# Which engine issues the context and V transfers beside the mixing stages: SyncE or ScalarE

## What is computed

```
x = L0(x, ctx)          # RWKV: mixing of neighbouring rows, recurrence over 112 steps, channel mix
x = L1(x, ctx, ctx)     # two cross-attentions of 16 heads x 128, then an MLP
x = L2(ctx, x, mask)    # attention of x over the context and itself, then an MLP
x = L3(x, ctx)          # attention of one head over the context

# of L0
x5  = xn[:, :, None] + sx[:, :, None] * (maa_stack + tanh(...) @ maa_w2)   # five mixes
r, k, v, g = x5[3] @ Wr.T, x5[0] @ Wk.T, x5[2] @ Wv.T, silu(x5[4] @ Wg.T)
s   = a + w * s ;  out = r . (u * a + s)                                   # a = k_t v_t
x   = x + (groupnorm(out) * g) @ Wo.T
kk  = square(relu(xk @ ffn_Wk.T)); x = x + sigmoid(xr @ ffn_Wr.T) * (kk @ ffn_Wv.T)

# of the first cross-attention of L1
vh  = (ctx @ wv1 + bv1).reshape(b, t, 16, 128)      # needs nothing of L0
```

## Time and profile before

| | |
|---|---|
| median of 3 runs | 3551.27 us |
| lowest, highest | 3536.88, 3551.39 us |
| the profiled execution: its time | 3549.67 us |
| its span | 3548.3 us |
| mean granted TensorE clock | 0.948 |
| busy: PE, DVE, ACT, POOL | 3189.4, 1486.5, 1238.4, 1109.2 us |
| chunk loads, V stores | 128 pairs, 96 |

### The profile page before, as it was taken

How to read it: one execution, slowest core, us unless ns; L and a number is a source line. 1 busy time by engine, 2 the same in 40 slices (tenths; PEclk the granted TensorE clock), 3 DMA queues, 4 the chain that set the end, 5 groups by cost and what they waited for, 6 DMA issues and landing times.

```text
span 3548.3 us, 43193 instructions
## 1 busy us (share of the span) xinstructions
PE 3189.4 (90%) x15928; PEld 2639.5 (74%) x15928; DVE 1486.5 (42%) x3184; ACT 1238.4 (35%) x2797; POOL 1109.2 (31%) x986
## 2 busy tenths in 40 slices
PE   5688978878699999999999999999899998988988
PEld 2454555556698989898989888888688777767876
DVE  4588349721333333343333333334211665662133
ACT  3222323232333333453222232223333555553322
POOL 5545335432322222332121121222342222234410
PEclk7799989989899999999999999999899999988999
DMA  6575357534333433342221121221111110101122
GB/s 226 173 217 160 118 164 223 160 110 135 117 130 122 139 128 117 129 141 73 81 86 65 65 94 65 83 80 49 36 60 58 37 37 23 39 15 54 57 82 91
DMA packets 142062, 358.25 MB, mean 101 GB/s; under 512 B 13008, under 2 KB 82128, under 8 KB 133024
## 3 DMA queue, kind: packets, MB, share of 16 engines
q1 hardware_dynamic: 141376, 354.81, 30.2%
q10 hardware_dynamic: 480, 0.69, 0.1%
HBM read 314.81 MB, written 40.63 MB: 100 GB/s over the span
## 4 chain that ended last, share of the span: by engine, by line
PE 66%; DVE 9%; ACT 7%; POOL 6%; DMA 6%; issue 4%; SPq 1%; POOLq 0%; ACTq 0%; DVEq 0%
PE bank L176 19%; PE bank L178 18%; PE bank L177 18%; PE bank L1728 5%; POOL W_lo L216 3%; DMA W_lo<-ctx_split 2%; PE bank L1713 1%; DMA W_raw<-in_weights 1%; ACT W_hi L207 1%; PE bank L620 1%; ACT prob L2408 1%; DVE prob_T_lo L256 1%; DVE max L1921 1%; ACT prob L1810 1%; DVE K_lo L258 1%
## 5 line engine op out<-in xcount | busy, mean ns | idle before, releaser
L2002 POOL TENSOR_SCALAR prob<-prob,inverse 112x376 f32<-112x376 f32 x256 | 143.5, 579 | 1124.6 <-DVE inverse L1927 1124.6
L216 POOL TENSOR_TENSOR W_lo<-W_raw,W_hi 128x1024 fp32r<-128x1024 f32 x138 | 331.1, 2421 | 192.6 <-ACT W_hi L207 190.3
L176 PE MATMUL bank<-ctx_hi,W_hi 128*128 128x376 f32 x1024 | 356.7, 348 | 26.0 <-DVE K_lo L258 20.2
L176 PE MATMUL bank<-W_hi 128*128 128x512 f32 (+2 forms) x608 | 282.8, 465 | 88.2 <-DMA W_lo<-ctx_split 49.8
L258 DVE SCALAR_TENSOR_TENSOR K_lo<-bank,vectors,K_hi 128x375 fp32r<-128x375 f32 (+1 forms) x288 | 173.8, 607 | 438.7 <-ACT K_hi L249 438.4
L177 PE MATMUL bank<-ctx_lo,W_hi 128*128 128x376 f32 x1024 | 346.0, 338 | 0.0
L178 PE MATMUL bank<-ctx_hi,W_lo 128*128 128x376 f32 x1024 | 345.4, 337 | 0.0
L176 PE MATMUL bank<-act_hi,W_hi 128*128 128x448 f32 x800 | 312.9, 391 | 29.0 <-POOLq L333 10.9
L177 PE MATMUL bank<-act_lo,W_hi 128*128 128x448 f32 x800 | 300.1, 375 | 0.0
L178 PE MATMUL bank<-act_hi,W_lo 128*128 128x448 f32 x800 | 299.8, 375 | 0.0
L249 ACT ACTIVATE K_hi<-bank,vectors 128x375 fp32r<-128x375 f32 (+1 forms) x288 | 163.4, 576 | 287.9 <-PE bank L178 287.8
(11 more groups left out here) (252 smaller groups left out, 6999.6 us busy)
## 6 DMA issues: line engine op xcount, KB each, us to landing
W_raw<-in_weights SPq DMA_DIRECT2D x69, 1024.0 KB, 5.0
ctx_hi<-ctx_split SPq DMA_DIRECT2D x64, 752.0 KB, 5.6
ctx_lo<-ctx_split SPq DMA_DIRECT2D x64, 752.0 KB, 7.1
v_spread<-v_rows SPq DMA_DIRECT2D x128, 224.0 KB
W_hi<-ctx_split SPq DMA_DIRECT2D x128, 188.0 KB, 3.3
W_lo<-ctx_split SPq DMA_DIRECT2D x128, 188.0 KB, 4.6
values<-value_rows SPq DMA_DIRECT2D x64, 256.0 KB
V<-values SPq DMA_DIRECT2D x32, 512.0 KB, 4.1
```

The source lines that it names most:

```text
L176: nc.tensor.matmul(dst, left[0], right[0], start=first, stop=False)
L216: pool.tensor_tensor(k.Wl[:, slot, cs, :], k.Wraw[:, cs, :], k.Wh[:, slot, cs, :].bitcast(F32), ALU.subtract).then_inc(*k.w_low.now((n, i)))
L2002: pool.tensor_scalar(k.Pm[:, h, :], k.Pm[:, h, :], k.rsum[:, h:h + 1], 1.0, ALU.mult, ALU.mult).then_inc(*k.prob_done.now((n, h)))
```

## The change

All chunk loads after those of the first context, and all stores of the V thirds, are issued by ScalarE. `act_fill` first loads the chunks that TensorE read at the point before, then stores the thirds that ScalarE copied out at the point before, then copies out as before. `act_values_end` stores as well. SyncE keeps the first context's chunks (`sp_first_chunks`), the weights, the spreads and the rest; its weight loads keep their places in the recurrences, and follow each other without fills between them in the mixing stage and in the channel mix. Nothing else moves: what is waited for, the lag of one point, the buffers and the transfers' shapes are the same.

```diff
 def act_fill(k, point):
     act = k.nc.scalar
+    for n in range(made_until(point, 2), made_until(point, 1)):
+        f, q = divmod(n, NQ)
+        j, c = QUANTA[q]
+        if j == 2 and f + 1 < len(FILLS):
+            act_chunk(k, f + 1, c)
+    for n in range(tiles_of(made_until(point, 3)), tiles_of(made_until(point, 2))):
+        act_value_store(k, n)
     for n in range(tiles_of(made_until(point, 2)), tiles_of(made_until(point, 1))):
         act_value_out(k, n)
...
 def act_values_end(k):
+    for n in range(tiles_of(made_until(POINTS[-1], 2)), tiles_of(made_until(POINTS[-1], 1))):
+        act_value_store(k, n)
     for n in range(tiles_of(made_until(POINTS[-1], 1)), len(TILES)):
         act_value_out(k, n)
+        act_value_store(k, n)
-def sp_fill(k, point):
...
-def sp_chunk(k, f, c):
-    sp, b = k.nc.sync, f % B
-    if f:
-        sp.wait_ge(*(k.chunk_read[f - 1, c] if c < C - 1 else k.banks.filled(("vf", f - 1, 2))))
+def act_chunk(k, f, c):
+    act, b = k.nc.scalar, f % B
+    act.wait_ge(*(k.chunk_read[f - 1, c] if c < C - 1 else k.banks.filled(("vf", f - 1, 2))))
     ch, cl = context_chunk(k, c)
-    sp.dma_start(ch.bitcast(F32), k.cx_dram[b, 0, :, c]).then_inc(k.chunk_loaded[c], 16)
-    sp.dma_start(cl.bitcast(F32), k.cx_dram[b, 1, :, c]).then_inc(k.chunk_loaded[c], 16)
+    act.dma_start(ch.bitcast(F32), k.cx_dram[b, 0, :, c]).then_inc(k.chunk_loaded[c], 16)
+    act.dma_start(cl.bitcast(F32), k.cx_dram[b, 1, :, c]).then_inc(k.chunk_loaded[c], 16)
-def sp_value_store(k, n):
+def act_value_store(k, n):
...
-    sp.wait_ge(*k.banks.drained(("vf", f, j)))
-    sp.dma_start(k.v1_dram[g, b, k0:k0 + kn], k.Vst[0:kn, n % 2, :]).then_inc(k.value_kept[n % 2], 16)
+    act.wait_ge(*k.banks.drained(("vf", f, j)))
+    act.dma_start(k.v1_dram[g, b, k0:k0 + kn], k.Vst[0:kn, n % 2, :]).then_inc(k.value_kept[n % 2], 16)
...
+def sp_first_chunks(k):
+    sp = k.nc.sync
+    for c in range(C):
+        ch, cl = context_chunk(k, c)
+        sp.dma_start(ch.bitcast(F32), k.cx_dram[0, 0, :, c]).then_inc(k.chunk_loaded[c], 16)
+        sp.dma_start(cl.bitcast(F32), k.cx_dram[0, 1, :, c]).then_inc(k.chunk_loaded[c], 16)
... in sp_rwkv:
             sp_load_weight(k, w["r"])
-            for s in range(14):
-                sp_fill(k, ("pre", 1, s))
-                if s == 5:
-                    sp_load_weight(k, w["v"])
-                if s == 10:
-                    sp_load_weight(k, w["g"])
-            sp_load_weight(k, w["o"])
+            for name in "vgo":
+                sp_load_weight(k, w[name])
...
-            sp_fill(k, ("rec", half, n))
... in sp_ffn:
-    for s in range(24):
-        sp_fill(k, ("ffn", s))
-        if s == 2:
-            sp_load_weight(k, W_FFN["fv"])
-        if s == 16:
-            sp_load_weight(k, W_X[0]["q"])
-    sp_values_end(k)
-    for w in "ko":
+    sp_load_weight(k, W_FFN["fv"])
+    for w in "qko":
         sp_load_weight(k, W_X[0][w])
```

More of the change, by code:

```diff
@@ L451, in act_values_end @@
 def act_values_end(k):
+    for n in range(tiles_of(made_until(POINTS[-1], 2)), tiles_of(made_until(POINTS[-1], 1))):
+        act_value_store(k, n)
     for n in range(tiles_of(made_until(POINTS[-1], 1)), len(TILES)):
         act_value_out(k, n)
-def sp_fill(k, point):
[L457 to L463, removed]
-def sp_chunk(k, f, c):
-    sp, b = k.nc.sync, f % B
-    if f:
-        sp.wait_ge(*(k.chunk_read[f - 1, c] if c < C - 1 else k.banks.filled(("vf", f - 1, 2))))
+        act_value_store(k, n)
+def act_chunk(k, f, c):
+    act, b = k.nc.scalar, f % B
+    act.wait_ge(*(k.chunk_read[f - 1, c] if c < C - 1 else k.banks.filled(("vf", f - 1, 2))))
     ch, cl = context_chunk(k, c)
-    sp.dma_start(ch.bitcast(F32), k.cx_dram[b, 0, :, c]).then_inc(k.chunk_loaded[c], 16)
-    sp.dma_start(cl.bitcast(F32), k.cx_dram[b, 1, :, c]).then_inc(k.chunk_loaded[c], 16)
-def sp_value_store(k, n):
-    sp, (f, j) = k.nc.sync, TILES[n]
+    act.dma_start(ch.bitcast(F32), k.cx_dram[b, 0, :, c]).then_inc(k.chunk_loaded[c], 16)
+    act.dma_start(cl.bitcast(F32), k.cx_dram[b, 1, :, c]).then_inc(k.chunk_loaded[c], 16)
+def act_value_store(k, n):
+    act, (f, j) = k.nc.scalar, TILES[n]
     (g, b), k0, kn = FILLS[f], KTILES[j][0], kept_rows(j)
-    sp.wait_ge(*k.banks.drained(("vf", f, j)))
-    sp.dma_start(k.v1_dram[g, b, k0:k0 + kn], k.Vst[0:kn, n % 2, :]).then_inc(k.value_kept[n % 2], 16)
-def sp_values_end(k):
-    for n in range(tiles_of(made_until(POINTS[-1], 2)), len(TILES)):
-        sp_value_store(k, n)
+    act.wait_ge(*k.banks.drained(("vf", f, j)))
[6 more added lines that the diff above has]
+        sp.dma_start(cl.bitcast(F32), k.cx_dram[0, 1, :, c]).then_inc(k.chunk_loaded[c], 16)
 def sp_learned(k):
@@ L1284, in sp_rwkv @@
                 sp.wait_ge(k.cx_stored[s], 32 * B)
-            for c in range(C):
-                sp_chunk(k, 0, c)
+            sp_first_chunks(k)
         pending = {}
@@ L1301, in sp_rwkv @@
                 sp_load_weight(k, pending[n])
-        if half:
-            sp_fill(k, ("post", 1))
 def plan_ffn(k):
```

## The result

| | before | after |
|---|---|---|
| median, lowest, highest of 4 runs, us | 3550.42 (3536.88, 3551.39) | 3603.31 (3600.66, 3606.64) |
| ratio, 95% interval | | 1.016 (1.014 to 1.018) |
| span and mean clock of the profiled execution | 3548.3 us, 0.948 | 3605.3 us, 0.940 |

The change makes the kernel 53 us slower. The prediction had said 26 us: the direction was right, the size was under half. The time is still inside the range on record. Two of the eleven executions of weights_later_again took 5985 and 7471 us and are left out of its ratio, not of its median.

A forecast was written before the change was run, and what follows sets the result against it. TensorE was taken to bound the mixing stages, with TensorE and VectorE close in the recurrences. Terms 21 + 11 + 6 - 10 - 10 - 4 + 12 = +26 us on the median 3551.3 gave 3577 us, range 3545 to 3615.

The forecast's parts named there:

- The rival that a DMA issue passes a waiting copy: ScalarE's loads go out while the copy ahead still waits, so all lateness is gone: about 3535 us; chance 0.05.
- the lateness: ScalarE's loads leave late behind waiting work: +21 us in the mixing stage, +11 us in the channel mix.
- the chunk behind the weight: Mixing stage: a chunk behind a 1 MB weight kept TensorE 4.52 us; in another queue it gains 4 us.
- the sign on record: Mixing stage: TensorE waits 25 us or more for chunks, in waits of 3 to 4 us, if the forecast is right.
- the step on TensorE's clock: Eight new stalls over 3 us each cost up to 3 us of low clock; half of 0 to 24 taken, +12 us.
- The even rival: Clock does not fall and mixing places overlap (15 instead of 21): +8 us, 3559 us; chance 0.24.
- the held loads: Recurrences: loads that SyncE issued late, at 491 and 515 us, go out earlier from ScalarE: -10 us.
- the queues: Recurrences: chunks in another queue need not stand behind spreads and weights: -10 us.
- The queue rival: A queue of its own saves chunks 1.5 to 2 us each: -24 us, 3527 us; chance 0.09.
- + 6: Recurrences: loads behind a gate or norm evacuation are 1 to 2 us late, four or five times: +6 us.
- issues and stores: 124 load pairs (93 us) and 96 stores (41 us) move into ScalarE's idle time and cost nothing themselves.
- the slowest rival: ScalarE's waits delay initial states, gates and V copies; 0.4 us per step, 128 steps: +51, 3628 us; chance 0.08.

The follow-up runs named there:

- weights_later_again: Kernel before with SyncE's g, fv and q weight loads asked for later, run again with more rounds: 3540.04 us, ratio 0.9981.
- loads_ahead_both: Changed kernel with ScalarE's loads and stores put ahead of the waiting copies in mixing stage and channel mix: 3557.50 us, 1.0032 of the kernel before.
- rec_only: Kernel before with the loads and stores of the two recurrences alone issued by ScalarE: 3549.18 us, ratio 1.0018.
- weights_later: Kernel before with SyncE's g, fv and q weight loads asked for at later points: 3537.99 us, ratio 0.9983.
- no_loads: Kernel before without chunk loads after the first context, whose chunks make the V of the seven others: 3507.69 us, ratio 0.9900.

## Why the prediction was right and where it failed

**Right: the place.** The prediction rested on ScalarE's order, in which each load stands behind a copy that waits for VectorE. The timeline shows it to 0.01 us, and loads_ahead_both, which moves the loads ahead of the copies in both stages, gives back four fifths of the loss. The rival that a DMA issue passes a waiting copy is refuted by the same rows. The Trainium skill (Advanced Engine Details and Errata, Sequencer Loop) lets an instruction of the engine wait in a queue while control instructions run; in this trace a DMA issue behind a waiting ScalarE copy did not run ahead of it, at 387.21, 397.70 and 408.00.

**Right: the lateness.** Forecast were 21 us for the mixing stage, less 4 for the chunk behind the weight: 17. TensorE's idle time rose by 15.9. Forecast for the channel mix were 11; it rose by 13.8. The sizes of single waits were off: eight waits in the mixing stage, as forecast, but one of 5.93 us and seven of 1.3 to 2.8, 21.2 us in all, where the sign on record was 25 us or more in waits of 3 to 4. The 9.40 us on a V copy became an 11.60 us wait for the chunk that now leaves behind eight copies, at 822.17. (The 3.9 us that the prediction had there are 3.8 by its own numbers.)

**Failed: the step on TensorE's clock, +12 us.** The mechanism was there and it was mis-sized: it is 25.1 us in the mixing stage and 8.2 in the channel mix, 33 in all. I had taken a price of up to 3 us from a single stall of 4.52 us with full work behind it, gave it only to stalls over 3 us, eight of them although its own average for the mixing stage was 2.7, and took half. The price held on the average: 25.1 us over the eight chunk waits of the mixing stage are 3.1 each. The half and the condition did not, since seven of the eight are under 3 us. Six of them come in pairs 7 to 8 us apart (392.84 and 400.59, 422.44 and 429.55, 481.61 and 489.37). At 400.59 the second wait ends before the clock has recovered from the first: 0.51 for 17 us at one go. Two short waits did the same, 1.65 us for a bank up to 441.88 and 1.36 us for a chunk up to 444.17. Behind them TensorE works without a stop and has the 1.2 GHz level for 12 us:

```profile
444.00:449.00 5.00, 4.83 (x8) 2.43 (x9) 0.00 (x0) 1.21 (x2) 0.00 (x0) 0.50 0.37 114
449.00:456.00 7.00, 7.00 (x16) 4.45 (x15) 0.00 (x0) 3.63 (x6) 0.00 (x0) 0.50 0.00 0
```

Even my upper bound of 24 was too low. The even rival, that the clock would hold as it did after waits of 1 to 2 us in the recurrences, failed with it.

**Failed: the reliefs in the recurrences, -10 for the held loads and -10 for the queues.** For the held loads the relief came and the time did not. The chunk waits of the second recurrence fell from 20.0 to 10.3 us and the longest from 5.2 to 2.5, close to the 10.4 that had been held up. For the queues not even the relief came. From issue to landing of the second load of a pair in the first and the second recurrence, before (135 to 340 and 487 to 698 us):

```profile
DMA to landing us min/median/max: 2.5/4.8/10.3
DMA to landing us min/median/max: 2.5/4.7/6.7
```

and after (135 to 341 and 529 to 743 us):

```profile
DMA to landing us min/median/max: 2.5/5.3/7.5
DMA to landing us min/median/max: 2.5/4.8/7.5
```

In rec_only it is 5.8 and 5.1 us. Over all pairs the median fell from 4.6 to 4.0 us, but that doesn't show a gain of the queue: by stages only the mixing stage has it (3.6 to 2.8, and 3.3 in the channel mix both times), and in weights_later, where SyncE issues every load, the median is 3.9. The queue rival, which needed 1.5 to 2 us for each landing, falls with it.

The two recurrences are 1 and 3 us longer, not 14 shorter as -10 - 10 + 6 says. VectorE is busy 90% and 87% of them, in the second TensorE's waits for GpSimd took the place of those for chunks (7.2 to 14.1 us), and no_loads bounds what any relief can give there at 9.8 us. The prediction had named VectorE's load as the limit and still counted 20 us.

**Right: issues and stores.** 78 of the 124 moved loads stand in the two recurrences, and rec_only costs 0.18%; the stores cost 0.22% even in all stages. The delayed initial states of the slowest rival, 51 us over the 128 steps, didn't come: the recurrences are 4 us longer.

**The sum.** By the traces: 15.9 + 13.8 idle, 25.1 + 8.2 clock, 4 in the recurrences make 67 us, against 17 + 11 + 12 - 14 = 26 forecast. The rest of the program takes off 10, and the 57 us between the two traces stand beside the 53 of the runs. Of the 41 us missing in the sum, 21 are the clock, 18 the reliefs, 2 the lateness.

## What to carry to other kernels

A DMA issue put on a compute engine inherits that engine's waits: look in its order at what stands ahead of each issue, and if it must move, put it ahead of the instruction that waits. Where TensorE sets the end, price a new wait twice, once as idle time and once as the products behind it at half the clock, and take neighbouring waits together. A wait removed in a stage that another engine sets is worth what that engine leaves; taking the transfers away altogether measures it.

## What was not expected of the hardware

- Chunk waits of 1.3 to 5.9 us, 21 us in all over a stage of 188, lowered its granted clock from 0.93 to 0.78 and cost more in slow products (25 us) than in idle time (16 us).
- Two waits of 1.65 and 1.36 us that ended 2.3 us apart were followed by 12 us at the 1.2 GHz level although TensorE worked all the time.
- 28 us of added zero products ahead of such waits kept the clock at 0.95, and the stage was no longer than without them.
- Chunks in a queue of their own landed no sooner beside the spreads of the recurrences: medians of 5.3 and 4.8 us against 4.8 and 4.7.
- The same order of the mixing stage gave 166.2 and 156.3 us in two traces, and four traces with its loads behind the copies gave 181 to 193: a stage length from one trace is good to about 10 us here, where medians of whole runs, 8 to 19 of them, tell 0.2 to 0.3% apart.
